# First and last batch on slot tables of their own, first inputs staged in idle tiles, and row maxima that wait for fewer writes

## What is computed

```python
qkv = x @ w_qkv + b_qkv            # 512 -> 8 * (64 q, 64 k, 64 v)
attn = softmax(q @ k.T / 8)        # per head, over 1024 keys
res = (attn @ v) @ w_out + b_out + x
```

## Time and profile before

| | us |
|---|---|
| median of 3 runs (lowest, highest) | 3923.45 (3922.22, 3924.38) |
| profiled execution | 3922.59 |
| span in the profile | 3920.8 |
| PE busy | 3823.5 (98%) |
| ACT, DVE, POOL busy | 3022.9, 2663.7, 1991.4 |

### The profile page before, as it was taken

The page is one execution under the profiler, slowest core; times in us unless marked ns, Lnnn a source line. Parts: engine busy times, 40 slices in busy tenths (PEclk is TensorE's granted clock), DMA queues, the critical chain, the costliest instruction groups (busy, mean ns, idle before and its releaser), DMA issues.

```text
span 3920.8 us, 97172 instructions
## 1 busy us (share of the span) xinstructions
PE 3823.5 (98%) x39180; PEld 3143.7 (80%) x39180; DVE 2663.7 (68%) x4379; ACT 3022.9 (77%) x5141; POOL 1991.4 (51%) x1030
## 2 busy tenths in 40 slices
PE   6999999999999999999999999999999999999998
PEld 5878788787888878888787888878878788787886
DVE  5776666666676676666666676676766666666665
ACT  5887877878777787777877788787887877878776
POOL 2454544545445464454644546455454544545444
PEclk9999999999999999999999999999999999999999
DMA  2011111111112121121111211112111110111111
GB/s 89 20 51 48 53 47 26 55 42 55 47 26 58 36 58 44 26 66 31 55 47 26 68 28 53 47 34 65 26 53 47 43 57 23 52 47 47 47 26 52
DMA packets 100722, 178.49 MB, mean 46 GB/s; under 512 B 16192, under 2 KB 16192, under 8 KB 100288
## 3 DMA queue, kind: packets, MB, share of 16 engines
q1 hardware_dynamic: 100288, 172.29, 15.7%
HBM read 71.57 MB, written 33.55 MB: 27 GB/s over the span
## 4 chain that ended last, share of the span: by engine, by line
PE 90%; DVE 4%; ACT 3%; issue 2%; DMA 0%; POOL 0%; SPq 0%; ACTq 0%; DVEq 0%
PE psum L494 36%; PE psum L513 13%; PE psum L544 11%; PE psum L546 11%; PE psum L566 6%; PE psum L570 6%; PE psum L568 6%; DVE max_parts L730 1%; PE psum L503 1%; ACT p_hi L644 1%; ACT p_full L643 1%; PE psum L521 1%; DVE q_shift L716 1%; ACT q_hi_hi L626 1%; DVE p_lo L749 0%
## 5 line engine op out<-in xcount | busy, mean ns | idle before, releaser
L410 POOL TENSOR_TENSOR p_lo<-p_full,p_hi 128x1024 f16<-128x1024 f32 x768 | 1646.1, 2144 | 1746.4 <-ACT p_hi L644 1745.4
L643 ACT ACTIVATE p_full<-psum,prob_bias 128x512 f32<-128x512 f32 x2048 | 1427.9, 697 | 672.0 <-PE psum L546 664.8
L730 DVE TENSOR_REDUCE max_parts<-psum 128x1 f32<-128x512 f32 x2048 | 1379.8, 687 | 737.0 <-PE psum L513 729.9
L644 ACT ACTIVATE p_hi<-psum,prob_bias 128x512 f16<-128x512 f32 x2048 | 1424.1, 695 | 0.0
L566 PEld LDWEIGHTS psum<-v_parts,p_hi 128*128 128x128 f16 x8192 | 744.5, 98 | 243.6 <-issue 153.9
L513 PE MATMUL psum<-k_lo_hi,q_hi_hi 128*128 128x512 f32 x2048 | 848.0, 435 | 25.2 <-issue 22.2
L566 PE MATMUL psum<-v_parts,p_hi 128*128 128x65 f16 x8192 | 858.8, 193 | 5.3 <-ACT p_hi L644 2.7
L568 PE MATMUL psum<-v_parts,p_hi 128*128 128x64 f16 x8192 | 852.7, 192 | 0.0
L570 PE MATMUL psum<-v_parts,p_lo 128*128 128x65 f16 x8192 | 850.2, 194 | 0.0
L544 PE MATMUL psum<-q_hi_hi,k_lo_hi 128*128 128x512 f32 x2048 | 806.0, 394 | 11.8 <-ACT p_hi L644 8.1
L546 PE MATMUL psum<-q_shift,k_shift 128*128 128x512 f32 x2048 | 801.9, 392 | 0.0
(11 more groups left out here) (59 smaller groups left out, 4721.8 us busy)
## 6 DMA issues: line engine op xcount, KB each, us to landing
x_in<-in_xT SPq DMA_DIRECT2D x128, 256.0 KB, 3.0
q_hi_hi<-q_hi_hi SPq DMA_DIRECT2D x256, 128.0 KB, 2.2
k_shift<-k_lo_hi SPq DMA_DIRECT2D x256, 128.0 KB, 2.3
y_tile<-in_x SPq DMA_DIRECT2D x128, 256.0 KB, 2.7
result<-y_tile SPq DMA_DIRECT2D x128, 256.0 KB, 2.0
o_heads<-in_L_conv_w_qkv SPq DMA_DIRECT2D x12, 256.0 KB, 4.1
o_heads<-in_L_conv_w_out SPq DMA_DIRECT2D x4, 256.0 KB, 4.9
out_bias<-in_L_conv_b_out SPq DMA_DIRECT2D x1, 256.0 KB, 4.3
```

The source lines that it names most:

```text
L410: nc.gpsimd.tensor_tensor(p_lo[:, g % LO_SLOTS, :, :], p_full[:, g % 2, :, :], p_hi[:, g % HI_SLOTS, :, :], ALU.subtract).then_inc(p_lo_re ...
L643: nc.scalar.activation(p_full[:, g % 2, n, :], scores(g, n), ACT.Exp, scale=SCALE, bias=prob_bias[:, :])
L644: nc.scalar.activation(p_hi[:, g % HI_SLOTS, n, :], scores(g, n), ACT.Exp, scale=SCALE, bias=prob_bias[:, :]).then_inc(exp_done, 1)
L730: nc.vector.reduce_max(max_parts[:, u % 2, q_tile, k_half:k_half + 1], bank(b, w), AX.X).then_inc(done["row_max"], 1)
```

## The change

1. The first batch has its own `v` table, its own `qk` slots for head 0 (slots -8 and -7, whole), and the slots begin at -8 instead of -17. Its eight `x` tiles are loaded at once into idle tiles (four in `p_full`, three in `y_tile`, one in `x_in`), and their low parts are subtracted on DVE instead of POOL. Weight parts 2 and 3 and the value bias are split within slots -5 and -4 instead of before the first slot; the output bias goes through `w_out` in slot -1.
2. The last batch has its own tables for transposes, projections and bias; its `y` has six places (`y_tile` and `x_in`).
3. For all batches the `v` table of heads 0 to 3 and the table of `x` splits move.
4. The row maxima wait for the keys' low part (L714) through a new semaphore, no longer for L716; `step_scores` waits for L716 instead. The copy of the queries' high part waits for L626 alone, that of the keys' as before.
5. `y` loads are issued three slots ahead of the bias, not four.

```diff
-X_SPLIT_SLOT = (-17, -17, -16, -15, -14, -14, -13, -12)
+X_SPLIT_SLOT = (-17, -16, -15, -15, -14, -13, -12, -11)
-V_SLOT = ((-13, -12, -9, -6, -5, -4, -3, -1), (11, 15, 18, 20, 23, 26, 28, 31))
+V_SLOT = ((-13, -12, -11, -9, -6, -5, -4, -3), (11, 15, 18, 20, 23, 26, 28, 31))
+FIRST_V_SLOT = (-6, -5, -5, -4, -4, -3, -1, 0)
+LAST_O_TRANSPOSE_SLOT = (62, 62, 62, 64, 66, 66, 67, 68)
+LAST_PROJECT_SLOT = (63, 63, 64, 65, 66, 67, 68, 69)
+LAST_Y_BIAS_SLOT = (54, 55, 56, 57, 58, 59, 67, 68)
...
+    if h == 0 and b == 0:
+        return [(begin + half, 0, TERMS)]
...
             weight_loads(0)
-            for n in range(X_SLOTS):
+            for n in range(CH_TILES):
                 x_load(0, n)
             weight_loads(1)
+            for n in range(CH_TILES, X_PARTS):
+                x_load(0, n)
...
-            for n in range(X_SLOTS, X_PARTS):
-                x_load(0, n)
             weight_loads(2)
             weight_loads(3)
+            for n in range(X_SLOTS):
+                x_load(1, n)
...
-                wait_work(sp, hi_done, b, ("qk", h, half))
+                wait(sp, q_hi_done, PER_BATCH["qk"] * b + rank(("qk", h, half)) + 1)
                 sp.dma_start(q_hi_hi[DIM:P, h % 2, cols].bitcast(f32),
                              q_hi_hi[0:DIM, h % 2, cols].bitcast(f32)).then_inc(q_hi_hi_ready[half], 16)
+                wait_work(sp, hi_done, b, ("qk", h, half))
...
-                wait_work(pe, done, b, ("qk", h, 1))
+                wait(pe, k_lo_done, PER_BATCH["qk"] * b + rank(("qk", h, 1)) + 1)
...
                     if half == 0:
+                        wait_work(pe, done, b, ("qk", h, 1))
                         for k in range(HALVES):
                             wait(pe, k_shift_ready[k], (HEADS * b + h + 1) * 16)
...
-                if g == 0:
+                if g == -1:
                     bias_through_w_out()
...
+            weights_hi(0)
+            for n in range(X_PARTS):
+                x_hi(0, n)
+            weights_hi(1)
...
+                if g == BEGIN_SLOT + 3:
+                    weights_hi(2)
+                if g == BEGIN_SLOT + 4:
+                    weights_hi(3)
+                    value_bias_hi()
...
+            weights_lo(0)
+            for n in range(X_PARTS):
+                dve.wait_ge(x_hi_done, n + 1)
+                hi, lo = x_part(n)
+                nc.vector.tensor_tensor(lo, x_stage(0, n), hi.bitcast(f32), ALU.subtract).then_inc(first_x_lo_done, 1)
+            weights_lo(1)
```

More of the change, by code:

```diff
@@ L59, with v_slot, project_parts, fills_of_slot @@
 MAX_TILES = (((0,), (1,)), ((2,), (3,)), ((4, 5), (6,)), ((7,), ()))
-def fills_of_slot(c):
+def v_slot(b, group, t):
+    return FIRST_V_SLOT[t] if b == 0 and group == 0 else V_SLOT[group][t]
+def project_parts(b, t):
+    return ((LAST_PROJECT_SLOT[t], 0, TERMS),) if b == BATCH - 1 else PROJECT_PARTS[t]
+def fills_of_slot(b, c):
     parts = []
@@ L65, in fills_of_slot, with completed_in_slot @@
         for half in range(HALVES):
-            parts += [(("qk", h, half), first, last) for at, first, last in qk_parts(h, half) if at == c]
+            parts += [(("qk", h, half), first, last) for at, first, last in qk_parts(b, h, half) if at == c]
     for group in range(2):
-        parts += [(("v", group, t), 0, TERMS) for t in range(TOKEN_TILES) if V_SLOT[group][t] == c]
-    parts += [(("project", t), first, last) for t in range(TOKEN_TILES) for at, first, last in PROJECT_PARTS[t] if at == c]
-    return parts
-def completed_in_slot(c):
-    return [w for w, _, last in fills_of_slot(c) if last == TERMS]
+        parts += [(("v", group, t), 0, TERMS) for t in range(TOKEN_TILES) if v_slot(b, group, t) == c]
+    parts += [(("project", t), first, last) for t in range(TOKEN_TILES) for at, first, last in project_parts(b, t) if at == c]
+    return parts
+def completed_in_slot(b, c):
+    return [w for w, _, last in fills_of_slot(b, c) if last == TERMS]
 def ring_early(c):
@@ L88, in ring_late, with transposes_of_slot, y_biases_of_slot @@
     return [("row_max", u, n // 2, n % 2) for n in MAX_TILES[at][1]] + ([("shift", u)] if at == 3 else [])
-def transposes_of_slot(c):
-    return [("o_transpose", t) for t in range(TOKEN_TILES) if O_TRANSPOSE_SLOT[t] == c]
+def transposes_of_slot(b, c):
+    slot = LAST_O_TRANSPOSE_SLOT if b == BATCH - 1 else O_TRANSPOSE_SLOT
+    return [("o_transpose", t) for t in range(TOKEN_TILES) if slot[t] == c]
+def y_biases_of_slot(b, c):
+    slot = LAST_Y_BIAS_SLOT if b == BATCH - 1 else Y_BIAS_SLOT
+    return [t for t in range(TOKEN_TILES) if slot[t] == c]
 def x_splits_of_slot(c):
@@ L183 @@
 SLOTS = [(g, [b for b in range(BATCH) if FIRST_SLOT <= g - STEPS * b <= LAST_SLOT + 2])
-         for g in range(FIRST_SLOT, STEPS * (BATCH - 1) + LAST_SLOT + 3)]
+         for g in range(BEGIN_SLOT, STEPS * (BATCH - 1) + max(LAST_PROJECT_SLOT) + 3)]
 def is_step(g):
@@ L254, in attention_block @@
         fixed_ready = sem("fixed_ready")
+        first_x_loaded = [sem(f"first_x_loaded{k}") for k in range(HALVES)]
         x_loaded = [sem(f"x_loaded{k}") for k in range(X_SLOTS)]
@@ L313, in x_number, with x_arrived @@
             return b * X_PARTS + n
+        def x_arrived(engine, b, n):
+            if b == 0:
+                engine.wait_ge(first_x_loaded[n // CH_TILES], 16 * CH_TILES)
+            else:
+                slot = x_number(b, n) % X_SLOTS
+                engine.wait_ge(x_loaded[slot], 16 * (x_number(b, n) // X_SLOTS + 1 - (X_PARTS + X_SLOTS - 1 - slot) // X_SLOTS))
         @block.sync
@@ L361, in y_load @@
             def y_load(b, t):
-                if t >= Y_SLOTS:
+                if b == BATCH - 1 and t >= LAST_Y_SLOTS:
+                    wait(sp, y_stored[t - LAST_Y_SLOTS], 16 * (b + 1))
+                elif b == BATCH - 1 and t >= Y_SLOTS:
+                    wait(sp, x_lo_done, (BATCH - 1) * X_PARTS)
+                elif t >= Y_SLOTS:
                     wait(sp, y_stored[t - Y_SLOTS], 16 * (b + 1))
@@ L375, in _ @@
                     c = g - STEPS * b
-                    for w in completed_in_slot(c):
+                    for w in completed_in_slot(b, c):
                         if w[0] == "qk":
@@ L428, in _ @@
                             x_lo(b, n)
-                    for t in range(TOKEN_TILES):
-                        if Y_BIAS_SLOT[t] == g - STEPS * b:
-                            y_bias(b, t)
+                    for t in y_biases_of_slot(b, g - STEPS * b):
+                        y_bias(b, t)
         @block.tensor
@@ L597, in x_hi, with weights_hi @@
                 x_free(act, b, n)
-                slot = x_number(b, n) % X_SLOTS
-                act.wait_ge(x_loaded[slot], 16 * (x_number(b, n) // X_SLOTS + 1))
-                nc.scalar.copy(x_part(n)[0], x_in[:, slot, :]).then_inc(x_hi_done, 1)
-            for part in range(W_PARTS):
+                x_arrived(act, b, n)
+                nc.scalar.copy(x_part(n)[0], x_stage(b, n)).then_inc(x_hi_done, 1)
+            def weights_hi(part):
                 act.wait_ge(weights_in[part], 16 * CH_TILES)
@@ L605, in _, with value_bias_hi @@
                     nc.scalar.copy(weight_part(part, c)[0], stage[:, stage_slot(part, c), :]).then_inc(w_hi_done, 1)
[L606 to L608 removed]
+            def value_bias_hi():
+                act.wait_ge(consts_in, 64)
+                act.wait_ge(fixed_ready, 1)
+                for c in range(CH_TILES):
+                    nc.scalar.activation(bias_hi[:, c, :], zeros, ACT.Identity, bias=v_bias[:, c:c + 1]).then_inc(w_hi_done, 1)
+            weights_hi(0)
+            for n in range(X_PARTS):
+                x_hi(0, n)
+            weights_hi(1)
             act.wait_ge(consts_in, 64)
[L611 to L613 removed]
             def transposed_hi(b, w):
@@ L677, in _, with weights_lo @@
             nc.vector.memset(k_shift[0:Q_TILES, :, :].bitcast(f32), 1.0).then_inc(fixed_ready, 1)
-            for part in range(W_PARTS):
+            def weights_lo(part):
                 for c in range(CH_TILES):
```

110 lines of the change are left out of this document (66 added, 44 removed).

## The result

The changed kernel takes 3898.15 us (median of 4 runs, 3897.42 to 3899.63) against 3923.06 for the kernel before (4 runs): a ratio of 0.9937, 95% interval 0.9919 to 0.9954. It is faster by 24.9 us. The forecast was 3877, a gain of 46.4; the measured time lies inside the range of 3859 to 3900, 1.85 us from its slow end. Two of the five parts came about as forecast, one had the wrong sign, and two fell short.

A forecast was written before the change was run, and what follows sets the result against it. PE, busy 98% of the span, was taken as the bound. Gains of 10.4 + 7.5 + 10.5 + 12.5 + 5.5 = 46.4 us, taken from 3922.59, gave 3876.2, plus 0.86 gave 3877 us; range 3859 to 3900.

The forecast's parts named there:

- Part A: Row maxima need L714, not L716: slot 35 gains 0.65 us a batch, slot 43 nothing; 10.4 us, bounds 0 and 24.
- Part C: `v` table moved: the `qk` fill's wait for L705 in slot 0 goes; 10.5 us, bounds 0 and 16.
- Part B: `x` splits moved: slots 47 and 50 lose a cast each, slot 49 gets two; gain 7.5 us, bounds -15 and +16.
- the five bounds: Bounds of the five parts, taken as independent; added as squares (10, 12, 7, 5, 3) they give some 18 us.
- This loss, 0.68 us from start to start, nearly goes: Scores at 1672.51 waited for the exponential behind two casts; with one cast fewer in slot 47, the 0.68 us nearly go.
- rival 2: Only the ends gain: parts A to C are eaten by ACT, continuously busy in slots 47 to 53; 3905; chance 0.13.
- rival 3: Slower: slot 49's pair of subtractions holds up POOL, PE loses 2.9 us a batch; 3949; chance 0.04.
- Part D: Start: PE begins at about 13, what began at 67.94 begins at about 55.4; gain 12.5 us, bounds 7 and 17.
- I take 28: Start: the copied queries, issued at about 23.4 behind loads, land at 28; alone a copy takes 2.2 us.
- fills and tiles: Start: from 28 PE has about 13 us of these, plus some 1.6 us waiting for DVE: scores of step 0 at 43.
- as before: Start: two low-clock losses of 2 us each counted, the same as in the kernel before.
- Part E: End: projections fill PE's 2.28 us wait, five 0.5 us waits and 0.7 of low clock go; 5.5 us, bounds 2 and 8.

The follow-up runs named there:

- shift_first_42: Changed kernel with DVE's low part of the queries (L795) behind the shift in slot 42 alone: 3897.62 us.
- x_late: Changed kernel with the last four `x` tiles split behind slot 51, by another `x`-split table: 3893.89 us.
- x_splits_back: Changed kernel with the `x`-split table of the kernel before: 3895.59 us.
- copies_first: Changed kernel with SP issuing the first head's copies of queries and keys ahead of later loads: 3892.17 us.
- bias_slots: Changed kernel with the last batch's first six biases in slots 47, 51 and 55, where POOL has no low part of probabilities: 3895.36 us.
- v_one_later: Changed kernel with the first three `v` fills of the next batch one slot later: 3922.73 us.

## Why the prediction was right and where it was wrong

The forecast's gain was 46.4 us; the medians show 24.9, the spans 24.5. By the profiled spans, A gave 10.1 and C 7.8 when made alone, B -3.1 by undoing it (3896.3 - 3893.2), the start 7.1 and the end 0.9: together 22.8.

By the sign that it set itself, the prediction's account of the middle was wrong: a batch had to become 1.5 to 2.5 us shorter, and it became 1.10. The third pair of scores was to come near 55 and came at 60.85. The other signs came: the waits for L705 and most of those for ACT gone, the first matmul at 12.95, and an end 4.7 us shorter. That the time still fell into the range is in part luck: the five bounds, added as squares, end at 3895, and 3898.15 is inside only because the range was drawn to 3900.

**Part A was right.** Forecast 10.4 from slot 35, measured 10.1 to 11.9 for the part alone. Also right was that slot 43 gains nothing, with L819 as the next wait. But the reason given, that the shift stands behind L795 on DVE, is only the upper layer: with the shift moved ahead (`shift_first_42`) the time stays, because ACT has no hole there. In slot 35 the prediction had asked that question and found ACT idle behind the wait; there the gain was real.

**Part C was right** in mechanism and near in size: forecast 10.5, measured 7.8 to 11.2 alone; the wait in slot 0 went, and the fill that arrived in slot -11 cost no more than it freed.

**Part B had the wrong sign**: forecast -7.5 us of time, found +2.6 to +3.1, inside its bounds. Two steps failed. "This loss, 0.68 us from start to start, nearly goes" held in its own slot: from the scores of step 49 to those of step 50 of batch 14 it is 4.65 us before and 4.09 after. But it took PE's wait for ACT as a matter of where the casts stand. ACT takes 12.2 us without a hole to the cast that slot 51's row maxima need, whichever table it follows (`x_late`), so PE comes sooner and waits there: step 51 went from 4.52 to 5.15 us. And the prediction asked whether POOL is late for the low parts of probabilities, but not who needs the `x` tiles: the `v` fill of slot -13, the last of whose four tiles is now the second of the pair in slot 49. That wait is the price: behind the keys' cast the changed kernel takes 0.29 us more than `x_splits_back`, about the 0.25 a batch that undoing the part gives. The prediction's words for rival 2 had the fact ("ACT, which is continuously busy in slots 47 to 53") and gave it 0.13 for parts A to C together; applied to B alone, it would have taken the gain away. The wait by which rival 3 was to be known, L628 for POOL, shows only in the last batch; POOL was the late engine, but at another place.

**Part D was mis-sized**: forecast 12.5, measured 7.1. The first matmul came at 12.95 as worked out (13). The copy was issued at 22.82 (forecast 23.4), but "I take 28" was 30.7 (22.82 + 7.90, the chain's row below), and the 15 us from there to the scores of step 0 were 18.2 (30.85 to 49.06). In `copies_first`, with the clock at 1.00, they were 17.1 (24.45 to 41.56), so the low clock behind the hole is about 1.1 of the 3.2; the other 2.1 were missing from the 13 us of "fills and tiles", since PE's waits for DVE there were 1.7 us (0.56, 0.76 and 0.42), as forecast. The prediction had counted the low clock behind two holes "as before", and none behind the wait that it had itself put there. `copies_first` gives that back: 53.38 for the third pair of scores, against the forecast 55.4.

```profile
22.82 7.90 DMA q_hi_hi<-q_hi_hi
```

The ring rule that the prediction cited (the Trainium skill, "DMA: Bandwidth & Descriptors", section on queues, rings and completion order: each DMA engine consumes descriptors in ring order) agrees with this: 7.90 us for the copy behind the loads, 2.2 alone, 2.3 when issued ahead of the fourth weight part (`copies_first`). No run tells the rule from plain load on the DMA engines, which were 0.88 busy while the copy waited.

**Part E was mis-sized**: forecast 5.5, about 0.9 left, below its bounds of 2 to 8. The gain behind the last exponential came (4.7), but the part never counted the biases: one a slot in slots 54 to 59, where POOL also has low parts of 2.14 us. Timeline of the changed kernel:

```profile
3849.31 0.69 ACT L708 ACTIVATE p_full<-psum,prob_bias 128x512 f32<-128x512 f32 x1 [0.90 <-POOL p_lo L471]
...
3852.63 0.69 ACT L708 ACTIVATE p_full<-psum,prob_bias 128x512 f32<-128x512 f32 x1 [0.90 <-POOL p_lo L471]
```

The two are one step apart, 3.32 us, about what a bias and a low part take together (1.28 + 2.14): POOL sets these steps. `bias_slots` shows 1.7 to 2.8 us of the 3.8.

## What to carry to other kernels

A wait on the busiest engine is worth its length only where the engine that would set the time next has a hole there; look for the next hole of each other engine ahead of and behind the wait, and compare the distance between holes. PE is busy 98% of this span, and yet ACT sets slots 42 to 45, and 48 to 51 up to the keys' cast, of every batch. Work for PE put into such a stretch can be free (0.9 us in slot 43), and work moved out of one gives back less than its length (1.1 of 1.4 us from slot 51) and costs where it arrives. When a result is made later, list all who read it, not only what its engine does next; and when a wait is put at a start, or work is taken out of a stretch in which PE waits, look at the granted clock behind it too.

## What the runs showed of the hardware

A subtraction of an `x` tile on POOL (L465) takes 1.287 us in the median of 120, but 2.09 where it began behind DVE's low part of probabilities (L828). Timeline of batch 14 of the changed kernel:

```profile
3579.06 1.23 DVE L828 TENSOR_TENSOR p_lo<-p_full,p_hi 128x1024 f16<-128x1024 f32 x1
3579.34 2.09 POOL L465 TENSOR_TENSOR xT_lo<-x_in,xT_hi 128x512 fp32r<-128x512 f32 x1 [3.79 <-ACT xT_hi L661]
```

The two overlap from 3579.34 to 3580.29, 0.95 us, and POOL lost 0.80. The Trainium skill, "Trainium Architecture — The Big Picture", section "What this means for kernel authors", says that DVE and GpSimd share a pair of ports under an exclusive lock; the trace agrees, and shows who pays. In the changed kernel 75 of the 120 subtractions don't overlap L828 and take 1.26 to 1.32 us. Thirty began behind L828 and took 2.09 in the median. In the other fifteen POOL began first: it kept its 1.27 to 1.29, and DVE's L828 took 2.07 in place of 1.23. The engine that came second lost about the time of the overlap. In the rows above the loss cost nothing further: POOL then waited 0.24 us for ACT.

Beyond that, the granted clock of 0.61 behind a hole of 6.3 us, and 1.00 without the hole, made a wait of 6.42 us cost 7.5. And it fell, to 0.69 over a step of 5.5 us, where PE had no hole longer than 1 us but was busy for only 2.70 of the 4.20 us of the step before (`v_one_later`, batch 6).
